# Block 0's queries before four value products, and the stacking of its heads before a weight load and the output weights' split

## What is computed

```python
x = x + xattn(layernorm(x), ctx_1024, Wq, bq, Wk, bk, Wv, bv, Wo, bo)
x = x + ffn(layernorm(x), W_experts, b_experts, W_router, b_router)
# xattn: q = x@Wq.T + bq; k, v from ctx; softmax(q k^T / sqrt(32)) v; @Wo.T + bo
# ffn:   top 2 of softmax(x@W_router.T + b_router); sum of those experts' linear outputs, weighted
```

## Time and profile before

| | |
|---|---|
| median of 3 runs | 1278.06 us (1278.04 to 1279.62) |
| profiled execution | 1286.87 us, span 1285.2 us |
| TensorE busy | 1196.6 us, 93% |
| VectorE busy | 877.4 us, 68% |
| ScalarE busy | 721.7 us, 56% |
| GpSimd busy | 743.1 us, 58% |
| mean granted TensorE clock | 0.971 of 2.4 GHz |

### The profile page before, as it was taken

How to read it: one execution, slowest core, us unless ns; L and a number is a source line. 1 busy time by engine, 2 the same in 40 slices (tenths; PEclk the granted TensorE clock), 3 DMA queues, 4 the chain that set the end, 5 groups by cost and what they waited for, 6 DMA issues and landing times. The chain is left out here.

```text
span 1285.2 us, 36001 instructions
## 1 busy us (share of the span) xinstructions
PE 1196.6 (93%) x11024; PEld 722.1 (56%) x11025; DVE 877.4 (68%) x1933; ACT 721.7 (56%) x1040; POOL 743.1 (58%) x980
## 2 busy tenths in 40 slices
PE   7987999999999999999999968899899999999997
PEld 4444666666666666666666645554455555555554
DVE  3765798888888879879887886455355555555554
ACT  3328756966876776786696564533333333333333
POOL 4004436766866865776677584866544454454445
PEclk9979999999999999999999987799899999999999
DMA  9853635865774674684576465969999899898886
GB/s 236 272 129 113 164 105 162 248 204 148 211 236 152 192 233 159 185 247 162 153 215 205 126 181 206 346 182 210 183 186 180 173 180 194 174 172 164 165 165 130
DMA packets 135546, 239.22 MB, mean 186 GB/s; under 512 B 18439, under 2 KB 49415, under 8 KB 134279
## 3 DMA queue, kind: packets, MB, share of 16 engines
q1 hardware_dynamic: 102391, 161.24, 42.9%
q0 software_dynamic: 29808, 67.73, 26.1%
q10 hardware_dynamic: 3232, 8.68, 1.9%
HBM read 112.00 MB, written 101.40 MB: 166 GB/s over the span
## 5 line engine op out<-in xcount | busy, mean ns | idle before, releaser
L1855 PE MATMUL S<-we_s,wq_s 128*128 x1620 | 374.4, 381 | 13.0 <-DVE wq_s L1811 6.2
L1783 POOL DMA_INDIRECT out<-xn,to x135 | 208.9, 1547 | 204.6 <-DMA out<-xn,to 122.5
L1855 PEld LDWEIGHTS S<-we_s,wq_s 128*128 128x128 f16 x1620 | 157.3, 98 | 179.8 <-issue 20.0
L1172 POOL TENSOR_TENSOR we_s<-P_s,we_s 128x1024 f16<-128x1024 f32 x96 | 203.9, 2137 | 55.5 <-ACT we_s L927 55.2
L1794 ACT ACTIVATE wq_s<-PVp 128x512 f16<-128x512 f32 x137 | 81.6, 596 | 248.3 <-PE PVp L1845 248.3
L975 DVE TENSOR_REDUCE mx_sb<-S 128x6 f32<-128x924 f32 x160 | 171.6, 1110 | 12.5 <-PE S L726 9.9
L746 PE MATMUL W<-wo_s,aT_hi 128*128 128x512 f16 x512 | 165.1, 384 | 2.6 <-DVE aT_lo L953 1.4
L708 PE MATMUL W<-we_s,wq_s 128*128 128x512 f16 x512 | 158.2, 386 | 5.6 <-DVE xnT_lo L953 3.4
L1833 DVE SCALAR_TENSOR_TENSOR att<-S,be_s 128x512 f32<-128x512 f32 x135 | 93.3, 691 | 97.6 <-PE S L1855 95.8
L1252 POOL DMA_INDIRECT dispatched<-xn,idx x128 | 131.7, 1029 | 44.6 <-issue 41.1
L1811 DVE TENSOR_TENSOR wq_s<-PVp,wq_s 128x512 f16<-128x512 f32 x137 | 94.5, 690 | 42.4 <-ACT wq_s L1794 42.4
(11 more groups left out here) (207 smaller groups left out, 2057.0 us busy)
## 6 DMA issues: line engine op xcount, KB each, us to landing
P_s<-dispatched SPq DMA_DIRECT2D x139, 260.5 KB, 3.9
we_s<-we_s SPq DMA_DIRECT2D x186, 128.0 KB, 6.2
be_s<-in_x SPq DMA_DIRECT2D x16, 1024.0 KB, 10.3
xR_s<-in_x SPq DMA_DIRECT2D x16, 1024.0 KB, 7.4
out<-xR_s SPq DMA_DIRECT2D x16, 1024.0 KB, 5.3
wst<-in_weT SPq DMA_DIRECT2D x16, 512.0 KB, 6.2
we_scratch<-wsp SPq DMA_DIRECT2D x16, 512.0 KB, 6.0
Kst<-k_scratch SPq DMA_DIRECT2D x16, 480.0 KB, 5.7
```

What stands on the lines that cost most here:

```text
L1172: e.tensor_tensor(Pst[1][:, r:r + 2, :], exps(n), Pst[0][:, r:r + 2, :], ALU.subtract).then_inc(pldp, 1)
L1783: e.indirect_dma_start(out, bass.IndirectOffsetOnAxis(ap=to[u][:, :], axis=0), yw[u % YW], None, bounds_check=N - 1, oob_is_err=False, com ...
L1855: m = e.matmul(Yp[:, u % 2, :], gT[u % 2][xp][:, k, :], we_s[:, bass.ds(n * WN + (wp * KC + k) * D, D)], start=(c == 0), stop=(c == 11))
```

## The change

For block 0 only:

- TensorE: the value products 1 to 4 are all done behind Q11; none stands ahead of XT2 and of Q0 any more.
- VectorE: the values 1 to 3 are taken after the low half of Q group 3, ahead of the low half of the output weights' split and of value 4. Value 0 stays ahead of Q group 0.
- ScalarE: the six DMA issues of heads 2 and 3 come before the high half of the output weights' split.
- SP: the six issues of heads 0 and 1 come before the next expert weights' load and the rows of block 3.

```diff
     def pe_XT(e, b, i, s):
         if b.first and i == 0:
             e.wait_ge(p_v32, 3)
-        if b.first and i == 2:
-            pe_value(e, 1)
...
     def pe_Q(e, b, i, s):
         if b.first and i == 0:
-            pe_value(e, 2)
             e.wait_ge(p_bk, 5)
...
         if b.first and i == 11:
-            pe_value(e, 3)
-            pe_value(e, B)
+            for bt in range(1, B + 1):
+                pe_value(e, bt)
...
     def act_Qh(e, b, G):
         if b.first and G == 3:
-            act_split(e, 2)
-
             e.wait_ge(qle, 4)
             restack_heads(e, b, (2, 3))
+            act_split(e, 2)
...
     def dve_Ql(e, b, G):
-        if b.first and G < 3:
-            dve_value(e, G)
+        if b.first and G == 0:
+            dve_value(e, 0)
         e.wait_ge(qhe, b.at(4, G + 1))
...
         if b.first and G == 3:
-            dve_value(e, 3)
+            for bt in range(1, B):
+                dve_value(e, bt)
             dve_split(e, 2)
             dve_value(e, B)
...
     def sp_slot(e, s):
         if on_b:
             sp_KV(e, b)
+        if b.first:
+            sp_RS(e, b)
         if on_bp1:
             sp_WL(e, bp1)
         if on_bp3 and bp3.past(3):
             sp_XA(e, bp3)
-        if on_b:
+        if on_b and not b.first:
             sp_RS(e, b)
+        if on_b:
             sp_WW(e, b)
             sp_MR(e, b)
```

More of the change, by code:

```diff
@@ L1685, in sp_slot @@
             sp_XA(e, bp3)
+        if on_b and not b.first:
+            sp_RS(e, b)
         if on_b:
-            sp_RS(e, b)
             sp_WW(e, b)
```

## The result

| | before | after |
|---|---|---|
| median of 20 runs each | 1278.05 us | 1282.66 us |
| ratio, 95% interval | | 1.0035 (1.0018 to 1.0051) |
| profiled execution, span | 1286.87, 1285.2 us | 1282.93, 1281.2 us |

What follows compares the result with a forecast made beforehand. TensorE's chain bounds the kernel, entered when VectorE's L999 starts. Stacking 0.2 us earlier, issues 5.47, high half 1.90, low half 2.20 and value 4 1.79 put L999 5.5 us later; clock -0.4: +5.1, 1283.1 us (range 1279.3 to 1287.0).

Steps and rivals of the forecast that it cites:

- The measure: Block 0's entry into TensorE's chain: set by the start of VectorE's L999, forecast 5.5 us later, 63.72 to 69.2.
- Part 2: ScalarE, block 0: L939's wait for its load eats the earlier queries' gain; 0.2 us left of 3.6 for the stacking.
- Part 3: ScalarE: the split's high half (1.90 us) now stands behind six issues, taken as 5.47 us, 4.1 for the range.
- Part 4: VectorE: low half (2.20 us) waits for ScalarE until 65.2, then value 4 (1.79), so L999 comes 5.5 us later.
- issues nearly free: Rival on ScalarE's DMA issues: they cost little, L999 +3.5 us less 0.4 for the clock, 1281.2 us; chance 6%.
- Part 1: TensorE, block 0: queries end at 50.4 instead of 53.98, but with idle gaps the four products end 3.3 us later.
- The cover: VectorE's value 4: its product is ready at 64.1, 3.3 us before needed, so a later TensorE would not show.
- The clock: TensorE's slow stretch in block 1's Q steps: -0.4 us, with +-1.5 us for the range.
- The rival of the early load: ScalarE not held by L939, so TensorE's order sets L999: +2.8 us less 0.4, 1280.5 us; chance 6%.
- The signs of being wrong: L939 well ahead of 52, L401 ahead of 61, or block 1's first score step under 3 us later with end unchanged.
- SP: SP's two loads go out some 7 us later and value stores 5.5 us later; cost nothing.
- Swallowed: Rival: slack further down the kernel absorbs the shift, 1278.5 to 1280.5 us; chance 12%.

Runs made afterwards that it cites:

- act_only: Kernel before with only ScalarE's swap: six DMA issues ahead of the high half of the output weights' split; ratio 1.0027 to before.
- dve_only: Kernel before with only VectorE's new order: values 1 to 3 behind the low half of Q group 3; ratio 1.0029 to before.
- sp_only: Kernel before with only SP's new order: issues of heads 0 and 1 ahead of the next weights' load and block 3's rows; ratio 0.9979 to before.
- after_again: The changed kernel run again, unedited, on another chip; ratio 1.0056 to the kernel before.
- best: Kernel before plus SP's new order, L939 and its remainder behind Q group 3, split behind block 1's transposes; ratio 0.9958 to before, 0.9988 when repeated.
- split_late: Changed kernel with both halves of the output weights' split moved far back, behind block 1's transposes; ratio 1.0026 to the kernel before.
- before_again: Kernel before run again without edit on another chip, for its profile; 11.12 us from L939 to L999, no ratio given.
- weh_after: Changed kernel with block 0's expert weights' split (L939 and its remainder) behind Q group 3 instead of Q group 1; ratio 1.0012 to the kernel before.
- no_act: Changed kernel with ScalarE's swap undone, high half of the split ahead of the six issues; ratio 1.0016 to the kernel before.
- best_q_first: Kernel best with the change's order on TensorE and of VectorE's values: queries first, products 1 to 4 behind; ratio 1.0038 to the kernel before.

## Why the prediction was right

- **The measure.** It took the start of L999 as what sets the entry of block 0. It moved by 4.69 us and the median by 4.6, and in every run the interval of the time holds the shift of L999 (5.47 us or 0.41% in act_only, 3.35 us or 0.25% in dve_only). That the two agree to 0.1 us is luck: the interval of the change is 2.3 to 6.5 us, and those of the experiments are no narrower.
- **Part 2** (the load eats the queries' head start) held: L939 waited 6.09 us, Q group 2 came 3.08 us after it, the stacking 0.24 us earlier against it (5.22 for 5.46; 0.2 forecast).
- **Part 3** was mis-sized in one term: issues of 4.65 us (55.93 to 60.58) in place of 5.47. The prediction named the reason, the 1 MB load that no longer goes out ahead of them, and left it to the range; sp_only bears it out. That is the whole of the 0.8 us between 5.5 and 4.69, since the stacking started 0.24 us earlier as forecast.
- **Part 4** held in its sizes: value 4 1.79, low half 2.21 us, no wait for product 4. But by the sum a reader would put the loss on the swap. The rival "issues nearly free" (+3.5) had the other half: without the swap 3.35 to 3.46 us stay. VectorE's chain was 1.2 us behind ScalarE's (2.0 by the text of part 4), and the sum should have said so.
- **Part 1** was right in the gaps (3.3 forecast, 3.54 in after_again), and the clock took no more than the 3 us that it allowed: 1.53 between the two traces of the changed kernel. The cover was smaller than it read. Value 4 started at 64.73; a value 4 that waits starts 0.20 us behind the first logits (57.75 and 57.55 in best), here at 62.85. So 1.88 us of the 3.3 were left, and 1.37 of them came from the preparation, which took 18.97 us from transpose 0 to L939 in place of 17.60. That the cover held is in part luck: the leg of split_late, 1.86 us longer, would have used it up.
- **The clock** behind it: -0.4 forecast, and MX0 moved 0.38 us less than L999 between the two traces used. Luck too: with before_again and after_again it is 0.25 to 0.73.
- **The rival of the early load** gave +2.8 by TensorE's order; weh_after shows +4.4 (15.51 - 11.12). Its arithmetic left out the low clock, some 2.9 us of TensorE's leg there (32.28 for 29.38).
- **The signs of being wrong** were written as times of one trace. Taken so, two of them came up: L939 started ahead of 52 (50.71) and L401 ahead of 61 (60.58). Counted from L939, L401 came 9.87 us after it, for 10.7 forecast and 8.4 as the limit. The signs should have been distances.
- **SP** cost nothing, as said. **Swallowed:** the medians show a loss as large as the shift of L999, within 2 us. The traces cannot show it, for the stretch from MX0 to the end scatters by 13 us between them (1240.7 to 1254.1 in the experiments).
- **Rule and trace.** The Trainium skill, "DMA: Bandwidth & Descriptors", section "Issuing engines are not separate DMA queues", has the issue time usually small beside the DMA. For one DMA the trace agrees, other than the prediction says: 0.81 us of issue in the median, 6.6 us to the landing. What costs is that six in a row hold the engine: in act_only the high half started 10.65 us after L939, behind 5.14 us of issues, not 4.22, and the time rose by 0.27%. The rule says nothing of work on the path that stands behind the issues.

What stays open: how much of sp_only's 0.21% is real and whether best gains anything beyond it, what keeps the clock up in best, and why the other chips are 3% slower. In the trace of before_again TensorE is busy for 504.83 of the 540 us from 200 to 740 us, against 521.46 in that of before, with most instructions as long (L708 and L746 379 ns in both, L786 397 for 380), a mean granted clock of 0.97 for 1.00, and 17.5 us of waits for L999 for 4.5.

## What to carry to other kernels

Work that an engine does "in between" is filler, and is worth as much as the gap that it fills: before moving it, find the gap, and ask what fills it afterwards. A step brought forward gains nothing if the next engine in its chain stands at a wait for a load, and even with the wait gone the next chain may end only a microsecond earlier and take its place; so write the end of every chain that meets at the bounding instruction beside its neighbours, not the latest alone. Where runs scatter by more than the effect, measure from an instruction that the change can't touch, look in every experiment whether it is still such a one (here four of them moved it), and measure from the start of each chain that can bind.

## What the runs showed of the hardware

Two gaps on TensorE of 1.2 to 2.1 us, 1 to 2 us of transposes between them, were followed by 1.2 GHz in five executions (the change, no_act, split_late, weh_after, best_q_first) but not in after_again, with gaps of 1.24 and 1.77 us; in the eight traces without these gaps the clock stayed at 2.4 GHz there. The leg took 30.91 to 32.77 us with the low clock and 29.38 without. Six DMA issues of 128 KB on ScalarE took 4.5 to 4.8 us (5.10 in one trace), and 5.1 to 5.4 with 1.5 MB of loads issued just ahead of them on SP; a single one landed after 4.4 to 4.9 and 6.5 to 6.9 us in the median. A leg of TensorE of 26 us without a wait repeats to 0.01 us, on chips whose whole times differ by 3%.
